# The order of the softmax maximum's matmuls within an attention step of a fused attention and mixture-of-experts block

## The reference

```python
x = x + tanh(g_xattn[0]) * xattn(layernorm(x), ctx_1024, ...)
x = x + tanh(g_ffn[0]) * ffn(layernorm(x), ...)
# xattn: 8 heads of 64; keys and values from 512 context rows (Wk2, Wv2) and 256 own rows (Wk1, Wv1)
sim = einsum('bihd,bjhd->bhij', q1, k) * scale        # 256 queries x 768 keys for each head
out = einsum('bhij,bjhd->bihd', softmax(sim), v)       # then @ Wo + bo
# ffn: gate with top 2 of 8 experts, and one shared expert; each 128 -> 512 -> gelu -> 128, all computed for all tokens
```

## Time and profile before

| | us |
|---|---|
| median of 3 runs | 157.04 (156.72 to 157.09) |
| the profiled execution, whole | 156.95 |
| its span, first to last instruction | 155.1 |
| PE busy | 143.9 (93%) |
| ACT busy | 115.1 (74%) |
| POOL busy | 107.9 (70%) |
| DVE busy | 103.5 (67%) |
| PEld busy | 111.4 (72%) |

### The profile page before, as it was taken

The page is one execution under the profiler, slowest core; times in us unless marked ns, Lnnn a source line. Parts: engine busy times, 40 slices in busy tenths (PEclk is TensorE's granted clock), DMA queues, the critical chain, the costliest instruction groups (busy, mean ns, idle before and its releaser), DMA issues.

```text
span 155.1 us, 4389 instructions
## 1 busy us (share of the span) xinstructions
PE 143.9 (93%) x1804; PEld 111.4 (72%) x1804; DVE 103.5 (67%) x215; ACT 115.1 (74%) x191; POOL 107.9 (70%) x95
## 2 busy tenths in 40 slices
PE   7789699979899999999898799999999999999992
PEld 5434354547566667657686698999999999989992
DVE  0779898888777686887763363834643779896631
ACT  3466789998988988887859988645567598968720
POOL 5506999777676667857798878965398089688730
PEclk9999999999999999999999999999999999999999
DMA  5679996000000000000000000030000000100001
GB/s 139 200 268 276 277 351 208 1 4 0 4 2 8 0 4 0 4 0 4 0 4 0 4 0 4 16 119 0 4 0 0 6 2 9 29 0 0 4 0 34
DMA packets 10253, 7.71 MB, mean 50 GB/s; under 512 B 1101, under 2 KB 8442, under 8 KB 10234
## 3 DMA queue, kind: packets, MB, share of 16 engines
q1 hardware_dynamic: 10234, 7.44, 15.8%
HBM read 7.18 MB, written 0.26 MB: 48 GB/s over the span
## 4 chain that ended last, share of the span: by engine, by line
PE 73%; DVE 10%; ACT 9%; issue 2%; DMA 2%; POOL 1%; SPq 0%; DVEq 0%; ACTq 0%
PE banks L1279 12%; PE banks L991 10%; PE banks L993 9%; PE banks L992 9%; PE banks L1242 5%; DVE part L821 4%; PE banks L1170 4%; ACT prob L646 3%; PE banks L1172 3%; PE banks L1171 3%; PE banks L1120 3%; PE banks L1190 2%; ACT v_hi L635 2%; DMA wf<-in_ctx_dram 2%; ACT p_hi L654 2%
## 5 line engine op out<-in xcount | busy, mean ns | idle before, releaser
L554 POOL TENSOR_TENSOR p_lo<-prob,p_hi 128x1024 f16<-128x1024 f32 x23 | 49.0, 2133 | 15.7 <-ACT p_hi L654 15.5
L710 ACT ACTIVATE prob<-banks,b1T 128x256 f32<-128x256 f32 x72 | 28.4, 475 | 12.8 <-PE banks L993 9.3
L646 ACT ACTIVATE prob<-banks 128x1024 f32<-128x1024 f32 x24 | 24.6, 1023 | 8.1 <-PE banks L1138 8.1
L821 DVE TENSOR_REDUCE part<-banks 128x2 f32<-128x1024 f32 (+1 forms) x24 | 29.0, 1216 | 1.1 <-PE banks L1093 1.0
L654 ACT ACTIVATE p_hi<-prob 128x1024 f16<-128x1024 f32 x24 | 25.4, 1057 | 0.8
L569 POOL TENSOR_TENSOR k_both<-prob,k_both 128x1024 f16<-128x1024 f32 x8 | 17.6, 2194 | 4.2 <-ACT k_both L718 3.2
L1279 PE MATMUL banks<-ring,prob 128*128 128x128 f32 x160 | 19.6, 276 | 0.0
L1170 PEld LDWEIGHTS banks<-v_hi,p_hi 128*128 128x128 f16 x192 | 17.4, 98 | 2.9 <-issue 2.5
L1170 PE MATMUL banks<-v_hi,p_hi 128*128 128x65 f16 x192 | 19.2, 195 | 0.0
L1171 PE MATMUL banks<-v_lo,p_hi 128*128 128x64 f16 x192 | 19.1, 193 | 0.0
L1172 PE MATMUL banks<-v_hi,p_lo 128*128 128x65 f16 x192 | 19.1, 194 | 0.0
(11 more groups left out here) (155 smaller groups left out, 343.8 us busy)
## 6 DMA issues: line engine op xcount, KB each, us to landing
ring<-in_L_ffn_w_dram SPq DMA_DIRECT2D x16, 256.0 KB, 5.3
wf<-in_ctx_dram SPq DMA_DIRECT2D x2, 256.0 KB, 5.3
ring<-in_L_xattn_Wk_dram SPq DMA_DIRECT2D x2, 256.0 KB, 4.7
ring<-in_L_xattn_Wv_dram SPq DMA_DIRECT2D x2, 256.0 KB, 7.1
ring<-in_L_ffn_ws_dram SPq DMA_DIRECT2D x2, 256.0 KB, 6.7
x_sb<-in_x_dram SPq DMA_DIRECT2D x1, 256.0 KB, 3.0
ring<-in_L_xattn_Wq_dram SPq DMA_DIRECT2D x1, 256.0 KB, 5.0
wo<-in_L_xattn_Wo_dram SPq DMA_DIRECT2D x1, 256.0 KB, 7.8
```

The source lines that it names most:

```text
L554: nc.gpsimd.tensor_tensor(p_lo[:, u % RINGP, :, :].rearrange("p a n -> p (a n)"), prob[:, u % RINGE, :], p_hi[:, u % RINGP, :, :].rearrang ...
L646: nc.scalar.activation(prob[:, u % RINGE, :], units(u).rearrange("p a n -> p (a n)"), ACT.Exp, scale=DH ** -0.5 / S_SCORE).then_inc(exp_do ...
L710: nc.scalar.activation(hid[:, k % NHID, c * T1:(c + 1) * T1], span(2 * (k % 2), HC * T1)[:, c * T1:(c + 1) * T1], ACT.Gelu, bias=b1T[:, e ...
L821: nc.vector.tensor_reduce(dst, src, AX_X, ALU.max).then_inc(part_done, 1)
```

## The change

On TensorE `max_chunk` moves from behind values and `shift_row` to directly behind the scores, in all steps from 0 on. Chunk 0 of pair 1, which was made in step -1 ahead of the first scores, is made in step 0 behind them, directly ahead of chunk 1. On VectorE, from step 0 on, `part_max` (and `whole_max`) moves ahead of the tails, `shift_out` and the normalisation of the same step, behind the low halves. In step -1 VectorE's order stays. Apart from this, entry 8 of `W2_STEP` goes: one copy of ScalarE and one subtraction of VectorE over 128 x 512 elements in steps 34 and 35, whose result nothing reads.

```diff
-W2_STEP = {2: FFN0 + 2, 3: FFN0 + 3, 4: FFN0 + 6, 5: FFN0 + 7, 6: FFN0 + 8, 7: FFN0 + 9, 8: FFN0 + 10}
+W2_STEP = {2: FFN0 + 2, 3: FFN0 + 3, 4: FFN0 + 6, 5: FFN0 + 7, 6: FFN0 + 8, 7: FFN0 + 9}
@@ VectorE
+            def chunk_maximum(p, c):
+
+                part_max(p, c)
+                if c == UPP - 1:
+                    whole_max(p)
+                if (p, c) == (0, UPP - 1):
+                    item_of(len(PRE) - 1)
+
@@ VectorE's loop
                 if i >= 0:
                     for n in items_at(i):
                         item_of(n)
+                if i >= 0 and chunk_of(i) is not None:
+                    chunk_maximum(*chunk_of(i))
                 for b, s in tail_of(i - 1):
                     tail(b, s)
...
                 if values_of(i) is not None:
                     reciprocals(values_of(i))
                     normalise(values_of(i))
-                if chunk_of(i) is not None:
-                    p, c = chunk_of(i)
-                    part_max(p, c)
-                    if c == UPP - 1:
-                        whole_max(p)
-                    if (p, c) == (0, UPP - 1):
-                        item_of(len(PRE) - 1)
+                if i < 0 and chunk_of(i) is not None:
+                    chunk_maximum(*chunk_of(i))
@@ TensorE's loop
             for i in range(CHUNK0, STEPS):
                 if 0 <= i < NU:
                     scores(i)
+                if i == 0:
+                    max_chunk(*chunk_of(-1))
+                if i != -1 and chunk_of(i) is not None:
+                    max_chunk(*chunk_of(i))
...
                 if values_of(i) is not None:
                     values(values_of(i))
                 if shift_of(i) is not None:
                     shift_row(shift_of(i))
-                if chunk_of(i) is not None:
-                    max_chunk(*chunk_of(i))
                 for n in late_items(i):
                     item_of(n)
```

## The result

The changed kernel takes 158.74 us in the median of 6 executions, the kernel before 157.04: 1.0126 times as long, with a 95% interval of 1.010 to 1.015 (the two medians by themselves give 1.0108). The forecast was 158.7 us in a range of 157.7 to 159.5. Single executions go from 158.29 to 160.04 us, those of before in the same comparison from 156.72 to 157.10. The longest one turned out to have a cause of its own, the clock.

What follows compares the result with a forecast made beforehand. PE's queue and its few waits were taken to bound steps 5 to 19, PE's own work from 89.3 us. Start +0.87, high half +1.83, steps 9/12/15 -0.60, reduction waits -1.38, copy +1.04: +1.76, forecast 158.7 us (157.7 to 159.5).

Steps and rivals of the forecast that it cites:

- Turns: Two fewer 64-row/128-row turns at 0.10 us each in eight counted steps; steps 9, 12 and 15 bring -0.60 us.
- Waits for the reduction: Steps 7 and 19: the chunk's wait of 0.69 us each for DVE's reduction goes, -1.38 us.
- The keys' high half: Steps 5, 8, 11, 14: chunk 0 waits for high halves made by ACT, 2.63 us, +1.83 net of turns.
- The tail's copy: Step 17: DVE's copy goes behind the reduction, PE's next transposes wait for it, +1.04 us net.
- The start: Steps 0 to 4: chunk 0 of pair 1 behind the first scores delays reduction, key projection and ACT, +0.87 us.
- The split: Steps 34 and 35: removing the unread copy and subtraction counts zero, since PE has no pause there; gain up to 0.6.
- Rival (c): Either the start's +0.87 or the copy's wait of +1.04 us is absorbed: 157.7 to 157.8 us; chance 0.14.
- Rival (b): Turns dearer than the starts show, break-even at 0.23 us each; at 0.27 the kernel takes 156.4 us; chance 0.05.
- Rival (d): DVE becomes the bound: `shift_out` late in steps 6, 9, 12, 15, or late normalisation, +0.8: 159.5 us; chance 0.06.
- Rival (a): The keys' high half is in time and costs nothing, `shift_out` comes late: 156.9 us; chance 0.07.

Runs made afterwards that it cites:

- a1_again: The changed kernel run once more, nothing altered, to count executions with a lower clock: 159.06 us, ratio 1.0142 to the kernel before.
- e3_key: Changed kernel with chunk 0 of pairs 2 to 7 back behind values and transpose, its reduction behind the normalisation: 157.25 us, ratio 1.0028 to before.
- e5_late: Changed kernel with batch 1's key projections one step earlier, value projections between them, bias transpose in step 15: 158.47 us, ratio 1.0085 to before.
- e2_tail: Changed kernel with VectorE's copies of the tails ahead of the reduction in each step: 157.73 us, ratio 1.0061 to the kernel before.
- e1_start: Changed kernel with chunk 0 of pair 1 back in step -1, ahead of the first scores: 157.49 us, ratio 1.0043 to the kernel before.
- e10_onlystart: Kernel before with only the start changed, chunk 0 of pair 1 behind the first scores: 158.25 us, ratio 1.0105 to before.
- e6_split: Kernel before without the dead split, entry 8 of `W2_STEP`, nothing else changed: 156.86 us, ratio 0.9997 to before.
- e4_three: Changed kernel with e1_start, e2_tail and e3_key together: 156.29 us, ratio 0.9958 to the kernel before.
- e9_middle: e4_three with VectorE's reduction of chunk 0 between `shift_out` and the normalisation instead of behind it: 155.14 us, ratio 0.9893 to the kernel before.
- e7_best: e5_late with the old start and the copies of the tails ahead of the reduction: 155.41 us, ratio 0.9903 to the kernel before.

## Why the prediction was right, and where not

The sum was +1.76 us, the medians differ by 1.70, and the traces, from the transposed maximum of step -1 to PE's end, by 1.64. That the median came within 0.04 us of 158.7 is in part luck: in a1_again, with two of six executions at the lower clock, the same kernel is 2.26 us over before, and the four others alone 1.79. The terms are what was right. Step by step, before against a1_again:

- **Turns.** Steps 9, 12 and 15 were to gain 0.60 us. They went from 3.26, 3.25 and 3.26 to 3.04, 3.04 and 3.05: -0.64. A turn costs 0.10 us, as read from the starts. The larger figure by the Trainium skill (TensorE: Matmul & The Clock Gate, Single matmul latency; 0.166 us, an estimate from its latency) is not what these steps show.
- **Waits for the reduction.** Steps 7 and 19: 2.97 to 2.28 and 3.87 to 3.17, -1.39 in all for -1.38. No wait for DVE's low half followed.
- **The keys' high half.** Steps 8, 11 and 14: 3.39, 3.37 and 3.45 became 3.98, 3.97 and 3.96, +1.70, where 0.58 + 0.59 + 0.52 was in the sum. Step 5 gave +0.07 instead of +0.14. e3_key and e5_late, which take the wait away in different ways, both lose it in just these steps, so this cause is shown.
- **The tail's copy.** Step 17: 3.22 to 4.26, +1.04 for 1.04. e2_tail removes it.
- **The start.** +0.88 us in the trace for +0.87. ACT's queue hands it on whole, as the prediction said: from the exponential of step 1 (22.50 before, 23.13 now) to that of step 5 it takes 12.15 us in both. e1_start and e10_onlystart bracket it from both sides.
- **The split.** Zero, as e6_split shows.

Steps 5 to 19 together: +0.76 for the +0.89 of the sum.

Rival (c), the absorbed start, fell with e1_start and e10_onlystart. Rival (b), dearer turns, fell with the lengths above (its own sum, by the way, gives 156.3 us for turns of 0.27, not 156.4). Rival (d) did not come in the steps that it named, where the cover of `shift_out` was 0.5 us. But `shift_out` was late once in the changed kernel, in step 3, which the prediction did not look at:

```profile
28.57 0.39 PE L1143 MATMUL banks<-shift,ones_row 64*128 64x256 f16 x4 [0.24 <-DVE shift L845]
```

It cost nothing, since ACT was the bound there and had no pause. And it appeared as soon as another wait went away: 0.22 us in step 18 of e2_tail. Rival (a), as made by e5_late, brought 1.54 us in steps 5 to 19, and there the copy's wait in step 17 is still in it.

Two things the prediction did not have. First, the clock: it noted a granted clock of 1.00 in every stretch and drew no case from what 0.87 us more of idle PE in step 0 could do to it. A fall costs 1.6 us in the trace (steps 0 to 4 take 18.98 us in the first profile and 17.34 in the second), and 1.1 in e3_key (18.46), where part of it lay in the idle stretch. With one such execution in the first six it hardly moved the median; it did decide the longest, 160.04, which is outside the range given for the median. Second, for what would be left if one cost were undone I counted the gains as independent. They aren't: in e3_key and e4_three the wait for the high half was exchanged for the wait for chunk 0's reduction, 1.4 us over steps 6, 9, 12, 15 and 18, by the difference between e3_key and e9_middle. The same failing stands behind the 43.1 us for e7_best, in which I had not put the exponential's hold on the score banks.

## What to carry to other kernels

Moving work forward in an in-order queue makes it meet its inputs sooner: look up, for each input, when it is ready against the new place, and count everything queued behind the wait. Here three of four costs were such meetings (the high half, the tail's copy, and at the start the reduction of the chunk that now came later), each readable from the trace of before to within 0.1 us. The meeting that only came up once another was gone (chunk 0's reduction) was not read there. The gains were had by moving only chunks 1 and 2 and ordering the other engine for the one wait that came up (155.14 us). Where engines start up by turns, a wait added there can also lower the clock in some executions (here 15 of 42), so look at the clock of each execution and not at the median alone. Scatter by itself doesn't tell: in a1_again executions with the full clock go from 158.22 to 159.26 us.

## What the runs showed of the hardware

- From 17.3 to 20.7 us PE was busy 2.47 of 3.40 us before; with the new start it was 1.68 of 3.43 us in the stretch that ends 0.3 us ahead of the fall. These are the rows of the changed kernel's first profile ahead of the fall, of before, and of a1_again, where the clock stayed up at nearly the same busy time (columns as in the earlier trace rows):

```profile
16.97:20.40 3.43, 1.68 (x21) 0.84 (x20) 2.53 (x4) 2.29 (x3) 3.43 (x4) 1.00 1.09 338
```

```profile
17.30:20.70 3.40, 2.47 (x27) 1.42 (x24) 3.40 (x5) 2.08 (x3) 3.40 (x3) 1.00 1.00 318
```

```profile
16.85:20.30 3.45, 1.67 (x21) 0.84 (x20) 2.56 (x4) 2.28 (x3) 3.45 (x4) 1.00 1.07 346
```

  The same program with the same gaps thus kept 2.4 GHz in one execution and went to 1.2 GHz for 3.41 us in another, although PE was at work all the time in which it was slow (3.41 of 3.41 us, 20.72 to 24.13). The gaps before, not the work in it, go with the fall.
- Matmuls of 64 rows next to matmuls of 128 rows cost 0.10 us at each turn, in either direction: from 64 to 128 rows by the starts of the earlier trace rows (0.32 us instead of 0.22), from 128 to 64 by the transpose, whose successor comes 0.24 us behind it when it is a chunk and 0.14 when it is a projection. Groups of the same shape follow each other without it. Steps 9, 12 and 15, which lost two turns each, got 0.21 to 0.22 us shorter.
